# Loading the tail's weights piece by piece during the experts, with one shared identity tile, in a transformer kernel on one Trainium2 core

## What is computed

```python
xn = _layernorm(x, axis=-1)
x = x + _L1_attn_ref(xn, ...) + _L1_ffn_ref(xn, ...)

# _L1_attn_ref: softmax attention, 16 heads of 16, then
x = x + attn_out                       # out @ Wo + bo
x_norm2 = layer_norm(x, g2, beta2)
ffn = jax.nn.relu(x_norm2 @ W1 + b1) @ W2 + b2
return x + ffn

# _L1_ffn_ref: shared expert and 8 routed experts, top 2 of 8 per row
shared = new_gelu(xf @ Wfc_s + bfc_s) @ Wproj_s + bproj_s
for e in range(N_EXPERTS):
    h = new_gelu(xf @ Wfc[e] + bfc[e]) @ Wproj[e] + bproj[e]
    routed = routed + h * gate[:, e:e + 1]
return (shared + routed).reshape(Bb, Tt, C)
```

## Time and profile before

| | |
|---|---|
| median of 3 runs | 4365.35 us (4365.05 to 4366.81) |
| profiled execution | 4365.6 us, span 4363.8 us |
| TensorE (PE) busy | 4100.0 us, 94% of the span |
| VectorE (DVE) busy | 3120.4 us, 72% |
| ScalarE (ACT) busy | 2660.6 us, 61% |
| GpSimd (POOL) busy | 367.7 us, 8% |
| DMA | 263.96 MB, 60 GB/s over the span |
| routed experts | 3298 to 3879 us, 39 tiles |

### The profile page before, as it was taken

How to read it: one execution, slowest core, us unless ns; L and a number is a source line. 1 busy time by engine, 2 the same in 40 slices (tenths; PEclk the granted TensorE clock), 3 DMA queues, 4 the chain that set the end, 5 groups by cost and what they waited for, 6 DMA issues and landing times. The chain is left out here.

```text
span 4363.8 us, 67013 instructions
## 1 busy us (share of the span) xinstructions
PE 4100.0 (94%) x23477; PEld 1781.2 (41%) x23748; DVE 3120.4 (72%) x4160; ACT 2660.6 (61%) x5113; POOL 367.7 (8%) x436
## 2 busy tenths in 40 slices
PE   6888739999999999999999999999998999999999
PEld 4666502222222222222222222222226888876666
DVE  6878579999999999999999999999940011132332
ACT  4555306788888888888888888888883233222222
POOL 0232350000110100000000000000002000011110
PEclk8999859999999999999999999999999999999999
DMA  4232354000005000004000002000005655522211
GB/s 152 78 105 80 116 95 80 4 23 22 23 27 99 21 9 6 4 4 81 6 4 4 6 4 72 6 3 4 6 3 156 216 185 195 199 81 77 73 54 37
DMA packets 209148, 263.96 MB, mean 60 GB/s; under 512 B 24881, under 2 KB 173617, under 8 KB 207313
## 3 DMA queue, kind: packets, MB, share of 16 engines
q1 hardware_dynamic: 198096, 233.17, 18.6%
q0 software_dynamic: 10752, 26.90, 2.1%
HBM read 184.76 MB, written 74.97 MB: 60 GB/s over the span
## 5 line engine op out<-in xcount | busy, mean ns | idle before, releaser
L1206 ACT ACTIVATE a_PT<-a_PS 128x512 f32<-128x512 f32 x4096 | 2114.7, 604 | 609.7 <-PE a_PS L1080 378.9
L1312 DVE TENSOR_REDUCE a_MX<-a_PS 128x2 f32<-128x1024 f32 x1062 | 1290.6, 1221 | 142.1 <-PE a_PS L1065 136.2
L1318 DVE TENSOR_REDUCE a_MX<-a_PS 128x1 f32<-128x512 f32 x1972 | 1266.1, 684 | 9.0 <-PE a_PS L1065 3.8
L1090 PE MATMUL a_OT<-a_PT,a_VG 128*32 128x512 f32 x8192 | 1091.7, 605 | 1.2 <-ACT a_PT L1206 0.8
L1080 PE MATMUL a_PS<-a_QS,a_KS 128*128 128x512 bf16 x1913 | 505.2, 381 | 30.3 <-issue 17.4
L1080 PE MATMUL a_PS<-p_Q,p_K 128*128 128x512 bf16 x1912 | 506.3, 382 | 24.8 <-issue 18.6
L1065 PE MATMUL a_PS<-p_K,p_Q 64*128 64x512 bf16 x2048 | 374.4, 401 | 51.8 <-DVE a_MX L1312 36.7
L1490 ACT ACTIVATE e_hT<-e_up,p_Q 128x256 f32<-128x256 f32 x312 | 148.0, 474 | 415.0 <-PE e_up L1443 414.9
L1065 PE MATMUL a_PS<-a_KS,a_QS 64*128 64x512 bf16 x2048 | 354.7, 384 | 2.4
L1065 PEld LDWEIGHTS a_PS<-p_K,p_Q 64*128 64x128 bf16 x2048 | 86.0, 93 | 580.6 <-ACT a_PT L1206 308.9
L1065 PEld LDWEIGHTS a_PS<-a_KS,a_QS 64*128 64x128 bf16 x2048 | 84.1, 93 | 530.8 <-ACT a_PT L1206 329.5
(11 more groups left out here) (233 smaller groups left out, 3425.7 us busy)
## 6 DMA issues: line engine op xcount, KB each, us to landing
p_K<-Wfc SPq DMA_DIRECT2D x26, 1024.0 KB, 5.0
p_K<-Wproj SPq DMA_DIRECT2D x26, 1024.0 KB, 7.1
p_Q<-Wfc SPq DMA_DIRECT2D x13, 1024.0 KB, 5.0
p_Q<-Wproj SPq DMA_DIRECT2D x13, 1024.0 KB, 7.1
scr_xs<-f_zero SPq DMA_DIRECT2D x1, 9984.0 KB, 32.8
p_Q<-scr_xs SPq DMA_DIRECT2D x39, 256.0 KB, 2.7
scr_ys<-e_Y SPq DMA_DIRECT2D x39, 256.0 KB, 2.2
f_X<-x SPq DMA_DIRECT2D x16, 512.0 KB, 4.7
```

What stands on the lines that cost most here:

```text
L1090: last = T.matmul(OT[w, :], VG[j][:, u, w], PT[:, (HG * u + h) % RING, :], start=u == 0, stop=u == KT - 1)
L1206: nc.scalar.activation(PT[:, c % RING, :], score_bank(c), ACT.Exp, scale=SOFT_SCALE).then_inc(S["exp_done"], 1)
L1312: V.tensor_reduce(MX[n % 2][:, :, x], PS[:, banks[0]:banks[0] + SIDES, :], AX.X, ALU.max).then_inc(S["mp_free"], SIDES)
L1318: V.reduce_max(MX[n % 2][:, side, x:x + 1], PS[:, banks[side], :], AX.X).then_inc(S["mp_free"], 1)
```

## The change

The tail's weights and its first two blocks' rows are still issued by GpSimd during the experts, but before each piece it waits until a certain number of tiles have done their ups (`tiles_begun(n)`): Wo at 3 tiles, the four 1 MB weights at 6, 9, 12 and 15, the seven small tensors all at 18. The rows of block i: piece k of `TAIL_IN` at tile 19 + 20 * (11 i + k) // 22, with no wait of their own before `DEN` and before `xT`. The three identity tiles become one, `pre["ident"]`, which attention fills; the memsets, selects and waits for it in the experts and the tail are gone.

```diff
@@ attention
-        identf = sb("identf", [P, P])
@@
+            identf = pre["ident"]
             nc.gpsimd.memset(identf[:], 0.0).then_inc(S["pchain"], 1)
@@ routed_experts
-        ident = sb("ident", [P, P])
+        ident = pre["ident"]
@@
-            nc.gpsimd.memset(ident[:], 0.0).then_inc(S["pchain"], 1)
-            pool.wait_ge(S["pchain"], 1)
-            nc.gpsimd.affine_select(out=ident[:], in_=ident[:], compare_op=ALU.not_equal, fill=1.0,
-                                    base=0, pattern=[[-1, P]], channel_multiplier=1).then_inc(S["ident_ok"], 1)
-            pool.wait_ge(S["up_done"], EBUF * HC)
-            tail_weights(pool, io, tt)
+            def tiles_begun(n):
+                pool.wait_ge(S["up_done"], n * HC)
+
+            tail_weights(pool, io, tt, lambda i: tiles_begun(EBUF + 3 * min(i, TAIL_BIG)))
             for i in range(2):
-                tail_rows(pool, scr, tt, i)
+                tail_rows(pool, scr, tt, i, lambda k: tiles_begun(TAIL_ROWS + (NTILE - TAIL_ROWS) * (i * TAIL_IN + k) // (2 * TAIL_IN)))
@@
-            pe.wait_ge(S["ident_ok"], 1)
             pe.wait_ge(load[0], LOADS * 16)
@@
+TAIL_BIG = 5
+TAIL_ROWS = EBUF + 3 * TAIL_BIG + 1
@@ tail_weights
+        ready(i)
         eng.dma_start(dst[:], src).then_inc(tt["w_load"], 16)
@@ tail_rows
+        ready(2 * G)
         eng.dma_start(tt["SUM"][j][rows, k, :], heads[:, 0:HD1, n]).then_inc(there, 16)
@@
+        ready(2 * NG + k)
         eng.dma_start(tt[name][j][:], scr[src][n, :].rearrange("(t p) c -> p t c", p=P)).then_inc(there, 16)
@@ tail
-        ident = sb("ident", [P, P])
+        ident = pre["ident"]
@@
-            nc.gpsimd.memset(ident[:], 0.0).then_inc(S["pchain"], 1)
-            pool.wait_ge(S["pchain"], 1)
-            nc.gpsimd.affine_select(out=ident[:], in_=ident[:], compare_op=ALU.not_equal, fill=1.0,
-                                    base=0, pattern=[[-1, P]], channel_multiplier=1).then_inc(S["ident_ok"], 1)
@@
-                if i == 0:
-                    pe.wait_ge(S["ident_ok"], 1)
@@ first_experts
+    pre["ident"] = ctx.enter_context(nc.sbuf_tensor("p_ident", [P, P], f32))
```

More of the change, by code:

```diff
@@ L1376, in sb @@
             return ctx.enter_context(nc.sbuf_tensor("e_" + name, shape, dt))
-        S = semaphores(nc, ctx, "e", "ident_ok pchain turned rows_ready up_done hid_ready "
+        S = semaphores(nc, ctx, "e", "turned rows_ready up_done hid_ready "
                  "down_done y_ready store0 store1 store2 spare")
@@ L1556, in tail_tiles, with tail_weights @@
     return tt
-def tail_weights(eng, io, tt):
+def tail_weights(eng, io, tt, ready):
     rows = lambda w: w.rearrange("(c p) n -> p c n", p=P)
-    for dst, src in ((tt["wo"], rows(io["Wo"])), (tt["wfs"], rows(io["Wfc_s"])), (tt["wps"], rows(io["Wproj_s"])),
+    for i, (dst, src) in enumerate(((tt["wo"], rows(io["Wo"])), (tt["wfs"], rows(io["Wfc_s"])), (tt["wps"], rows(io["Wproj_s"])),
                      (tt["w1"], rows(io["W1"])), (tt["w2"], rows(io["W2"])),
@@ L1564, in tail_weights @@
                      (tt["bob"], io["bo"].partition_broadcast(P)), (tt["b2b"], io["b2"].partition_broadcast(P)),
-                     (tt["bpb"], io["bproj_s"].partition_broadcast(P))):
+                     (tt["bpb"], io["bproj_s"].partition_broadcast(P)))):
+        ready(i)
         eng.dma_start(dst[:], src).then_inc(tt["w_load"], 16)
@@ L1571, in rows_load, with tail_rows @@
     return (tt[f"early{i}"], TAIL_IN * 16) if i < 2 else (tt[f"load{i % 2}"], i // 2 * TAIL_IN * 16)
-def tail_rows(eng, scr, tt, i):
+def tail_rows(eng, scr, tt, i, ready=lambda k: None):
     j, n = i % 2, slice(i * BLK, (i + 1) * BLK)
@@ L1579, in tail_rows @@
         heads = scr["att"][G].rearrange("(h w) n -> h w n", h=HG)
+        ready(2 * G)
         eng.dma_start(tt["SUM"][j][rows, k, :], heads[:, 0:HD1, n]).then_inc(there, 16)
         eng.dma_start(tt["DEN"][j][rows, k, :], heads[:, HD1:HD1 + 1, n].to_broadcast([HG, HD1, BLK])).then_inc(there, 16)
-    for name, src in (("XN1", "xn1"), ("RES", "resid")):
+    for k, (name, src) in enumerate((("XN1", "xn1"), ("RES", "resid"))):
+        ready(2 * NG + k)
         eng.dma_start(tt[name][j][:], scr[src][n, :].rearrange("(t p) c -> p t c", p=P)).then_inc(there, 16)
@@ L1600, in sb @@
             return ctx.enter_context(nc.sbuf_tensor("u_" + name, shape, dt))
-        S = semaphores(nc, ctx, "u", "pchain ident_ok chain bias_ok a_filled a_drained w_filled w_drained d_filled d_drained "
+        S = semaphores(nc, ctx, "u", "pchain chain bias_ok a_filled a_drained w_filled w_drained d_filled d_drained "
                  "rstd_in rstd_out z_ready mixed y_load0 y_load1 out_store")
@@ L1654, in _ @@
         def _(pool):
-            nc.gpsimd.memset(ident[:], 0.0).then_inc(S["pchain"], 1)
+            nc.gpsimd.memset(mhalf[:], -0.5).then_inc(S["pchain"], 1)
             pool.wait_ge(S["pchain"], 1)
-            nc.gpsimd.affine_select(out=ident[:], in_=ident[:], compare_op=ALU.not_equal, fill=1.0,
-                                    base=0, pattern=[[-1, P]], channel_multiplier=1).then_inc(S["ident_ok"], 1)
-            nc.gpsimd.memset(mhalf[:], -0.5).then_inc(S["pchain"], 1)
-            pool.wait_ge(S["pchain"], 2)
             for i in range(NB):
```

## The result

The changed kernel took 4346.35 us (median of 5 runs, 4344.48 to 4347.72) against 4366.81 us (median of 5 runs, 4365.05 to 4371.34) of the kernel before in the same comparison: a ratio of 0.995, 95% interval 0.9939 to 0.9962, so 20.5 us or 0.5% less. The prediction was 4344.8 us with 4340 to 4352 as its range. The profiled execution took 4344.48 us (span 4342.7), 21.1 us less than that of before.

A forecast was written before the change was run, and what follows sets the result against it. TensorE sets the experts' pace, with loaded DMA right behind, where a 10.12 MB burst stalls it. Spreading 20.3 plus identity 0.5, others 0, sum to 20.8 us: 4365.6 - 20.8 = 4344.8 us, range 4340 to 4352.

The forecast's parts named there:

- The spreading: Experts: pacing the tail's loads at 18 waits removes two DMA stalls and the slow running after them, 20.3 us less.
- Rival A: Experts' loads: the burst is not what delays the fetch, only the identity's 0.5 us remains; about 4365 us, 5%.
- Rival B: Experts: one tile still stalls, at the small tensors or at rows issued together, half the gain left; about 4355, 2%.
- Rival D: Experts: every large piece stalls its tile, deciding from a 9.9 us fetch delay on; 4424 or about 4371 us, 3%.
- my 0 to 3.5: Experts' loads: a 1 MB piece pushes a fetch back by 0 to at most 3.5 us, against 9.9 of slack.
- The identity at the start: Experts' start: TensorE no longer waits for GpSimd's identity tile, 0.5 us less, bounds nothing and 0.7.
- my bound of 0.7: Experts' start: upper bound on the gain from dropping the identity there, the whole of it, 0.7 us.
- The identity in the tail: Tail: its memset and select go, but the tile is first needed six steps in, off the path; 0 us.
- the shifted addresses: Attention: the shared tile shifts the large tensors by 512 bytes per partition, no transfer or instruction changes shape; 0 us.
- my reading of 4.5 us: Experts: slow running after the two stalls, 2.0 and 2.5 us lost, on top of 15.5 us of waiting.
- Rival C: Experts' start: the restart after attention keeps its clock as idle time shrinks to 3.3 us, 3.5 us more; about 4341, 3%.

The follow-up runs named there:

- the late burst: Changed kernel with all 34 tail transfers issued at once when 18 tiles had done their ups, not 3; 4365.56 us, ratio 1.0001 to the kernel before.
- the two bursts: Changed kernel with all weights (4.9 MB) issued at 3 tiles and all rows (5.2 MB) at 21; 4354.5 us, ratio 0.9977 to the kernel before.
- the identity alone: Changed kernel with the shared identity kept, but every piece of the tail's loads waiting for 3 tiles only; 4365.81 us, ratio 1.000 to the kernel before.
- the extra products: Changed kernel plus unread TensorE products after attention and after the experts: 10 and 10, 4343.14 us (0.9947); 10 and 6, 4340.35 us (0.9939).

## Why the prediction was right

*1. The spreading, 20.3 us.* Confirmed to the tenth in the account (by run times alone the whole change is known to about 5 us, from the interval), and shown to be the cause: alone it gives the gain, without it the gain is absent, moved it moves the stalls, halved it gives stalls of a third of the size (5.6 us for 15.5, in the fastest of its executions). Rival A (the burst is innocent) is ruled out by the late burst and the two bursts. Rival B (one tile still stalls) did not occur, in the change or with a piece in every tile. Rival D (each 1 MB piece stalls) falls by the landing at 9.3 us: a delay of 2.2 us, inside my 0 to 3.5 and far from the 9.9 that it needed. But 3.5 us was not the most: the small tensors, which I had counted as less than 1 MB, made a fetch 4 us late. The slack is what saved the forecast there.

*2. The identity at the start, 0.5 us.* The first turn came 0.52 us sooner after attention's end: it starts 4.33 to 4.35 us after attention's last products began in all seven traces with the shared tile and the meeting point as it was, 4.85 and 4.86 in the two with a tile of its own. That it stands at 3297.81, the very time forecast, is luck, as attention's end moves more than that. What the step left out is the clock behind it. The second turn comes 15.5 to 15.7 us after attention's last products in six of those seven traces (17.1 in the late burst) against 17.5 and 17.6, so the step gave 1.9 us at its place, above my bound of 0.7. In the change 1.2 of this was lost again at the tail. No median shows any of it.

*3 and 4. The identity in the tail and the shifted addresses, 0.* From the projection to the end the tail lost only the 1.2 us of its first products' clock, so the third term holds. For the addresses the runs show no cost, but only as finely as they can: attention's end moves by 8 us over the traces whatever the addresses, and the medians of the identity alone and of the kernel before differ by 0.3 us with an interval of about 4 us to either side.

*The clock.* I had counted it only with the stalls. It also moved at both meeting points, by 1.4 us for and 1.2 against. That they cancelled, and that the forecast is within 0.3 us of the profiled execution, is luck. For the stalls my reading of 4.5 us stands: the pitches lost 20.3 us with 15.5 of waiting. The estimate worked out from the Trainium skill, page "TensorE: Matmul & The Clock Gate", section "HAM oscillation — how this bites in real kernels", had 1.7 us of clock for the two stalls and 17.5 us in all, which is too little for this kernel. Rival C (the restart after attention keeps its clock at 3.3 us of idle time) did not occur in the change. The run with the late burst shows that it can, at the other meeting point: in its timeline

```profile
3881.50 3.69 PE L1696 MATMUL u_w<-t_wo,t_attT 128*128 128x256 f32 x16 [3.30 <-PEq L1374]
```

the projection ran at full speed after an idle time of 3.30 us. The granted clock of the stretch is 1.00, where that of the change was 0.50 after the same idle time:

```profile
3881.00:3885.00 4.00, 3.50 (x16) 3.14 (x17) 2.34 (x3) 0.00 (x0) 2.73 (x3) 1.00 0.08 22
```

```profile
3860.00:3864.00 4.00, 3.86 (x9) 3.17 (x10) 1.64 (x2) 0.00 (x0) 2.93 (x3) 0.50 0.12 37
```

That the range reached to 4340 for it was right; that I called the row of 5.38 us evidence against it was too strong, from one sample.

## What to carry to other kernels

A prefetch for a later stage is hidden only as long as it leaves the current stage's loads their slack: compare its bytes, at the rate of a full DMA, with what is free per step and with how early each load is issued. Leave a margin, since many small transfers can cost more than their bytes (4 us for 0.4 MB here). Here 1 MB per 14.25 us tile was free of charge and 5 MB at once already stalled TensorE, and a semaphore that the consumer counts anyway is enough to pace the issues. Put such prefetches on another queue than the urgent loads, since ahead of them on their own queue was the worst place of those tried; behind them on it was not tried.

## What the runs showed that I had not expected

After the same idle time of 3.3 us the first projection of the tail (16 passes) took 3.69, 5.38 and 6.55 to 6.60 us in different runs: whether and when the clock comes back is not settled by the idle time. It is worth up to 2.9 us at the tail's start and 3.4 at the experts' (from the first turn to the second 9.33 us with the extra products, 12.77 in the late burst). With the extra products the tail's clock stayed up in both runs, where it did in one of nine without; at the experts' start it stayed up in one of two, where it did in none of nine. That is few runs for a rule.

Single DMA issues of SyncE took 11.05 us under the burst where 0.44 is usual. With the burst on SyncE's own queue the 34 issues took from 3346.89 to 3388 us. That the fetch was issued so late goes a long way to explain why the stall was 13 us longer than bytes and slack had said. What holds such an issue, a full queue for instance, no view here shows.
